# GNN residual blocks with scatters and gathers by GpSimd: three of TensorE's counts moved from the last product to a drain instruction behind it

## The reference

```python
edge_index = jnp.stack([src, dst])
x = _layernorm(x + L0(x, edge_index, edge_attr_8, ...))
x = _layernorm(x + L1(x, src, dst, ...))

# L0: row, col = edge_index
h = silu(edge_rbf @ W1 + b1)                    # 8 -> 128 per edge
weights = h @ W2 + b2                           # 128 -> 128 per edge
messages = node_feats[col] * weights
aggregated = segment_sum(messages, row)         # by source
out = concat([node_feats @ Wself + bself, aggregated]) @ Wcat + bcat

# L1: segment means over both directions, then a GRU cell
a_in  = seg_mean((h @ W_in.T + b_in)[src], dst)
a_out = seg_mean((h @ W_out.T + b_out)[dst], src)
h = gru(concat(a_in, a_out), h)
```

## Time and profile before

| what | value |
|---|---|
| median of 3 runs | 8651.19 us (8642.64 to 8704.52) |
| the profiled execution | 8592.66 us, span 8591.0 us |
| TensorE busy, mean granted clock | 4860.7 us (57%), 0.685 |
| GpSimd busy | 5270.2 us (61%) |
| VectorE busy, ScalarE busy | 3136.4 us (37%), 1682.3 us (20%) |

### The profile page before, as it was taken

How to read it: one execution, slowest core, us unless ns; L and a number is a source line. 1 busy time by engine, 2 the same in 40 slices (tenths; PEclk the granted TensorE clock), 3 DMA queues, 4 the chain that set the end, 5 groups by cost and what they waited for, 6 DMA issues and landing times.

```text
span 8591.0 us, 115667 instructions
## 1 busy us (share of the span) xinstructions
PE 4860.7 (57%) x27117; PEld 4156.9 (48%) x27117; DVE 3136.4 (37%) x6639; ACT 1682.3 (20%) x4659; POOL 5270.2 (61%) x6008
## 2 busy tenths in 40 slices
PE   5888888888888899122232322323344444444337
PEld 4777777777777799122222322323233333333333
DVE  7555555555555567111111311112111111111128
ACT  2222222222223366100000000000111111111006
POOL 2556555555655676656666666665666666666654
PEclk7666667676767799566666666666666666666668
DMA  3222223222222598222222122221222222222225
GB/s 107 91 90 97 93 90 96 92 93 93 95 91 93 170 310 276 67 43 46 46 46 46 42 46 46 47 47 37 55 63 62 64 62 63 62 64 62 51 60 159
DMA packets 903626, 722.39 MB, mean 84 GB/s; under 512 B 601771, under 2 KB 703782, under 8 KB 902874
## 3 DMA queue, kind: packets, MB, share of 16 engines
q1 hardware_dynamic: 628082, 338.08, 14.6%
q0 software_dynamic: 161968, 341.31, 13.7%
q10 hardware_dynamic: 113469, 41.94, 1.9%
HBM read 556.95 MB, written 170.31 MB: 85 GB/s over the span
## 4 chain that ended last, share of the span: by engine, by line
another core or an unknown queue 34%; issue 11%; PE 9%; ACTq 4%; DVE 3%; ACT 2%; DVEq 2%; DMA 1%; POOL 0%; SPq 0%; POOLq 0%
PE bank L1966 5%; PE bank L2015 2%; DVE acc_b L1656 1%; ACTq L418 1%; DVEq L418 1%; DMA arena<-blktab 1%; ACTq L1035 1%; DVE acc_a L396 0%; ACT arena L1052 0%; ACTq L1066 0%; ACT acc_a L1014 0%; ACTq L1038 0%; DVE arena L1650 0%; PE bank L2071 0%
## 5 line engine op out<-in xcount | busy, mean ns | idle before, releaser
L821 POOL DMA_INDIRECT arena<-x1d,edge x3322 | 3142.5, 946 | 1741.9 <-issue 968.8
L2015 PE MATMUL bank<-arena 128*128 x8256 | 1438.7, 346 | 2245.4 <-DVE acc_b L1656 1575.9
L2015 PEld LDWEIGHTS bank<-arena 128*128 128x128 f32 x8256 | 1369.7, 257 | 2345.2 <-issue 2326.9
L762 POOL DMA_INDIRECT msgs<-arena x1664 | 1646.3, 989 | 1249.3 <-DVE arena L1436 774.5
L1650 DVE TENSOR_TENSOR arena<-bank,arena 128x1024 f32<-128x1024 f32 x516 | 631.2, 1224 | 3893.1 <-remote 3289.5
L1052 ACT ACTIVATE arena<-edge,arena 128x4 f32 x1032 | 224.7, 286 | 3159.7 <-issue 2951.4
L1916 PE MATMUL bank<-w2s,acc_b 128*128 128x128 f32 x3328 | 744.7, 392 | 20.1 <-issue 19.7
L1916 PEld LDWEIGHTS bank<-w2s,acc_b 128*128 128x128 f32 x3328 | 631.0, 282 | 160.6 <-issue 160.6
L1899 PE MATMUL bank<-arena 128*128 (+1 forms) x3328 | 662.8, 352 | 76.4 <-issue 72.8
L1899 PEld LDWEIGHTS bank<-arena 128*128 128x128 f32 x3328 | 585.5, 258 | 95.1 <-issue 92.6
L1401 DVE TENSOR_TENSOR_SCAN acc_b<-arena,acc_b 128x512 f32<-128x512 bf16 x415 | 531.7, 1281 | 7.4
(11 more groups left out here) (320 smaller groups left out, 5334.4 us busy)
## 6 DMA issues: line engine op xcount, KB each, us to landing
arena<-msgs SPq DMA_DIRECT2D x512, 272.0 KB, 4.9
arena<-rows SPq DMA_DIRECT2D x208, 512.0 KB
arena<-x1d,edge POOLq DMA_INDIRECT x3322
msgs<-arena POOLq DMA_INDIRECT x1664
pred<-arena ACTq DMA_DIRECT2D x98, 256.0 KB
arena<-pred SPq DMA_DIRECT2D x12, 1792.0 KB, 8.5
arena<-xwin SPq DMA_DIRECT2D x208, 64.0 KB
arena<-in_edge_attr_dram SPq DMA_DIRECT2D x207, 32.0 KB
```

What stands on the lines that cost most here:

```text
L762: pool.indirect_dma_start(msgs, bass.IndirectOffsetOnAxis(ap=pos[:, b, j:j + 1], axis=0), mrow[:, b, j, :], None).then_inc(scattered[b], 16)
L821: pool.indirect_dma_start(grow_t[:, sl, 0:D], None, x1d, bass.IndirectOffsetOnAxis(ap=edge2[:, odd * RING + sl, 1:2].bitcast(i32), axis=0) ...
L2015: last = mm(sum_at(q, u), oh1[:, q % 2, u * UT + k, :], rows[:, k * CW:(k + 1) * CW], start=(k == 0), stop=(k == UT - 1))
```

## The change

The counts place_ready, w_ready and sum1_ready are no longer incremented by the last product but by a drain instruction of TensorE that stands right behind it. All other counts of TensorE (attr_tr, h_ready, xj_ready, x_t, pre_lin and so on) stay on their products. Nothing is computed differently.

```diff
                 for j in range(TG):
                     last = mm(places_at[:, j:j + 1], place[0:NBP, b, j * P:(j + 1) * P], ones[0:NBP, 0:1], start=True, stop=True)
-                last.then_inc(s["place_ready"], 1)
+                pe.drain().then_inc(s["place_ready"], 1)
...
                 for k in range(4):
                     last = mm(bank[2 + h][:, k * P:(k + 1) * P], ht[:, b, h, k * P:(k + 1) * P], w2s[:, :], start=False, stop=(k == 3))
-                last.then_inc(s["w_ready"], 1)
+                pe.drain().then_inc(s["w_ready"], 1)
...
                         for k in range(UT):
                             last = mm(sum_at(q, u), oh1[:, q % 2, u * UT + k, :], rows[:, k * CW:(k + 1) * CW], start=(k == 0), stop=(k == UT - 1))
-                    last.then_inc(s["sum1_ready"], 1)
+                    pe.drain().then_inc(s["sum1_ready"], 1)
```

## The result

The changed kernel is slower: a median of 9491.35 us (9473.08 to 9493.97, 4 runs) against 8653.43 us (8642.64 to 8704.52, 4 runs) for the kernel before, a ratio of 1.0951 with a 95% interval of 1.0906 to 1.0996. Its profiled execution took 9490.72 us.

A forecast was written before the change was run, and what follows sets the result against it. No engine was taken as full: GpSimd's pause for late-reported TensorE counts set the edge period. 8592.66 + 280 (edge) + 310 (sums) = 9183 us profiled; with 58.5 us to the median, 9240 us, range 7700 to 9600.

The forecast's parts named there:

- late drains: On TensorE, a drain ends only when the products before it are reported, which is late while GpSimd issues indirect DMAs.
- The sums, +310 us: Second block's sums: the third pair of units waits for the second's report, 0.6 us per pair; ends 0 and +655.
- The edge phase, +280 us: Late places' drain uncovers weights(g, 0): 14.7 us per group, +1.35 us x 208; ends -30 and +500.
- GpSimd's run: Edge phase: eight indirect DMAs of a group, taken as 10.2 us.
- the release of L1455: Edge phase: from GpSimd's last DMA to VectorE's L1455, 0.1 to 1.6 us per group.
- a call of weights: Edge phase: weights(g, 0) runs only after the places' drain, 1.4 to 2.5 us per group.
- the step to GpSimd's next DMA: Edge phase: from VectorE's L1436 to GpSimd's start, 1.5 us per group.
- The drain's own cost: Lost overlap of products on TensorE in both stages, apart from late reports: taken as 0, 190 us kept for the range.
- The first rival: Drains end on time: edge phase -280 us, sums -600 us, median 7770 us; chance 0.34.
- The second rival: Drain late, but uncovered weights call mostly under landing messages and sums unaffected: 8560 to 8740 us; chance 0.14.
- The third, worse: Stopped TensorE becomes the edge phase's bound, +450 to +670 us, sums +655, up to 9900 us; chance 0.07.
- the likeliest case: Drain late and slower in edge phase and sums: 8780 to 9600 us; chance 0.52, third rival's 0.07 included.

The follow-up runs named there:

- uncounted drains: Kernel before with counts left on the last products and a drain that counts nothing behind each of the three (places, weights, second sums); ratio 1.0827 on the late chip.

## Why the prediction was right, and where its sizes were off

**Sign and mechanism.** Slower, by late drains: right. 9240 us was predicted, 9491 measured, inside the range of 7700 to 9600 and the likely one of 8780 to 9600; the loss of 838 us is 1.4 times the 589 us that were forecast over the median then known. All of what the profile after was to show is there: L1455 still waits for GpSimd's pause, L1914 comes after L1455, the pause of GpSimd is 5.7 us (5.5 in the mean, where it was 3.2), L2015 comes in runs of 16, the clock falls from 0.69 to 0.64 in the edge phase.

**The sums, +310 us.** Measured +306, and +256 to +268 in the runs with that drain alone, with uncounted drains, and without scatters (with drains against without). GpSimd's wait ahead of its gathers grew from 1741.9 to 2037.8 us, the same 296 us. The mechanism is there: in the changed kernel 195 of the 516 drains ended over 0.3 us after the last product (by up to 39.1 us) and had the next product of TensorE start within 0.6 us of their end, so they held it back. The size is in part luck. It was a choice of 0.6 us between 0 and 1.27, and 516 times the price of emptying TensorE found above, 0.64 to 0.67 us, would be 330 to 346 us, just as near. The prompt chip doesn't tell the two apart. There the drains end 0.02 us after their products and the sums lose nothing (4130.0 against 4134.2 us), but GpSimd's gathers are the bound by themselves (1017.1 us of idle time, 1012.6 of it their own gap), so a restart would be hidden as well.

**The edge phase, +280 us.** This is the term that was mis-sized; measured +592, 16.20 us per group ((3493.1 - 139.8) / 207) where 14.7 was forecast. The forecast added GpSimd's run, the release of L1455 behind it, a call of weights and the step to GpSimd's next DMA. The same four parts, as means over groups 20 to 199 of the traces, in us:

| part | forecast | before | changed | uncounted drains |
|---|---|---|---|---|
| GpSimd's eight DMAs, first start to last end | 10.2 | 10.18 | 10.76 | 10.73 |
| from there to L1455 | 0.1 to 1.6 | 0.77 | 1.17 | 0.55 |
| L1455 to L1436 | 1.4 to 2.5 | 0.98 | 2.83 | 2.84 |
| L1436 to the next DMA | 1.5 | 1.44 | 1.47 | 1.47 |
| the group | 14.7 | 13.35 | 16.23 | 15.59 |

The weights call came out over its upper end: TensorE's next product starts 0.26 us after the drain's end (median), and the call itself runs at the 1.2 GHz level (granted clock 0.50 from 1521.30 to 1524.00 us; 0.58 and 2.08 us in the group shown, 0.38 and 1.16 at full clock). The release is inside its range, but near the upper part, and 0.62 us later than with uncounted drains; that is the 0.65 us per group named there. It isn't the drain's own count that takes this time, since L1455 starts 0.04 us after the end of the drain: the report of the places itself comes later, 2.9 us after the last product in the mean where it was 2.1, and why isn't shown. The third is GpSimd's run, which the forecast held at 10.2. The traces show what lengthens it:

```profile
1529.23 1.72 POOL L762 DMA_INDIRECT msgs<-arena  x1 [0.30 <-issue]
...
1530.10 0.73 DVE L1430 TENSOR_SCALAR arena<-arena,iota_c 128x1024 f32<-128x1024 bf16 x1
```

The DMA ends at 1530.95, 0.12 us after VectorE's L1430 (1530.83). In the changed kernel 193 of the 1664 scatters take over 1.3 us, in the kernel before 51; in 192 and 40 of them L1430 runs meanwhile, and they end 0.12 to 0.13 us after it in nearly all. What they take beyond 0.96 us is 152 us in all against 31 us, which is the 119 us. A scatter that begins together with L1430 keeps its 0.96 us (1504.08 in the kernel before, beside an L1430 of 1504.06). So the change shifted VectorE's work against GpSimd's run, to where one scatter of nearly every group is held: a term that the prediction had at nothing.

**The drain's own cost, taken as 0 with up to 190 us kept.** As an instruction it costs nothing (13 ns). Emptying TensorE costs 0.64 to 0.67 us at full clock, not the 0.16 us of lost overlap that the earlier trace rows gave: the restart gap of 0.40 us was missing. It is paid where the products behind the drain are on the path, as in the first sums, and in the edge phase in full once nothing else is slower: +424 us without GpSimd's scatters and +451 us on a prompt chip. That TensorE waits anyway was true of the kernel before on a late chip only.

**The first rival, faster (0.34).** It took the drain as ending when the array is empty. It would have needed the drain behind the places to be about as long as their products; that is so on a prompt chip (2.17 us), and even there the change loses 6%, since TensorE is the bound. On a late chip it was 4.44 us. What the rival needed, a drain that is over before the products' count, isn't there: in the run with uncounted drains the two come within 0.01 us of each other. The Trainium skill, "Perfetto Trace Analysis", section "Per-instruction lifecycle", has the sequencer push a drain's increment once the drain's execution is complete, and a product's pushed on PSUM's acknowledgement; it doesn't say how long the drain executes, and here that is until the products are reported. The Trainium skill, "PSUM — Partial Sum Buffer", section "Engine vs sequencer instructions", has a drain wait until the engine is fully idle, and the trace agrees. **The second rival, no change,** fell, since the uncovered weights call lies wholly in GpSimd's pause. **The third, worse,** gave the edge phase's size (15.5 to 16.6 us) but not the sums', and by another way: it made TensorE's round the bound, while the parts in the table are those of GpSimd's.

**Slips in the prediction's sums.** The ends of the first rival, 7320 to 8230 us, hold the 58.5 us twice; over the median of 8651 they are 7260 to 8170. The third rival's upper end is 8651 + 670 + 655 = 9980 us, not 9900, and the low end of the likeliest case 8620, not 8630. None of them changes the account.

**What stays open.** Why one chip reports late and another doesn't, under the same kernel, isn't settled; one chip was late and two were prompt, and nothing here says what differs between them. That GpSimd's indirect DMAs are a condition of it is shown by the run without them. Whether it is GpSimd's issuing or the queue's work behind it isn't told apart. Nor is it shown that the results stood ready in PSUM before the count came: the end of a product's record is modelled, and no run reads the data ahead of the count, so a late write and a late report look the same here. That the clock adds its share in the edge phase is argued from windows, not isolated.

## What to carry to other kernels

Leave the count on the product that makes the data. A drain didn't make the count earlier, it waited for the same reports, and it took away the work that would have been issued meanwhile. Price it by what is queued behind it on the critical path (2.45 us per group here, nothing where there was slack), and by some 0.65 us for each time TensorE is emptied where TensorE is the bound. And before a wait is blamed on an engine, compare the end of its products with the start of the waiter: a distance that follows another engine's DMAs is not the products' run time. Last, when a change shifts engines against each other, look at how long the same instruction takes before and after: GpSimd's scatters grew by 119 us in a change that left them alone.

## What the hardware showed that I had not expected

- The kernel before takes 8590 to 8666 us on one chip and 7280 to 7293 us on two others. On the latter no late count of TensorE shows under GpSimd's indirect DMAs: L1650's wait is for the products themselves (3041.7 of 3114.8 us), and GpSimd's gathers wait 1017.1 us before them, nearly all of it their own gap, for 1741.9 (from the run with the places' drain behind the weights, whose sums are as before).
- On a prompt chip GpSimd is nearly the bound of the edge phase: its idle time ahead of L762 is 659.6 us, 510.7 of it its own gap (the run with the places' drain behind the weights), where it is 1249.3 us on the late chip. These 590 us, 2.8 us per group, are the distance from 13.35 to 10.64 us. That the kernel without scatters takes 10.54 us on the late chip has another reason: there TensorE is the bound.
- A drain is over when the count of the products ahead of it arrives (0.01 us from it in the median, in the run with uncounted drains). On a prompt chip it ended 0.02 us after their last record, on the late chip up to 40.0 us.
- A scatter of GpSimd's in which VectorE's L1430 starts 0.55 us or more after the scatter's own start ends 0.12 us after L1430 does, with 1.72 us instead of 0.96 in the case shown.
- Emptying TensorE costs 0.64 us per time at full clock, 0.24 us of it lost overlap and 0.40 us restart; a drain right behind another takes 13 ns.
- Three drains per group bring TensorE's granted clock from 0.80 to 0.67 although it is busy 92% and 90% of the time (the kernels without scatters).
